# Reordering ScalarE's queue in a cross-attention loop, and moving one projection unit behind each turn of X

## The reference

```python
x = layernorm(x + rwkv_block(x))               # recurrence over the tokens, and a gated MLP
x = layernorm(x + memory_attention(x, ctx))    # one head over causal own tokens and the context
x = layernorm(x + mixture_top1(x))             # 8 experts, 128 -> 512 -> 128
x = layernorm(x + sparse_attention(x))         # 16 heads of 8
x = layernorm(x + cross_attention(x, ctx))     # 16 heads of 64, keys and values from ctx
x = layernorm(x + mixture_top2(x))             # 8 experts with capacity 40
# cross attention:
Q, K, V = proj(x, Wq, bq), proj(ctx, Wk, bk), proj(ctx, Wv, bv)
attn = softmax(einsum('bhqd,bhkd->bhqk', Q, K) / sqrt(64))
out = einsum('bse,de->bsd', einsum('bhqk,bhkd->bhqd', attn, V), Wo)
```

## Time and profile before

| | us |
|---|---|
| three timed runs | 1335.52, 1335.23, 1333.54 |
| their median | 1335.23 |
| the profiled execution, its own time | 1334.87 |
| its span, first to last instruction | 1332.8 |
| mean granted TensorE clock | 0.973 |
| PE busy / DVE busy / ACT busy / POOL busy | 1178.3 / 736.7 / 697.5 / 153.9 |

### The profile page before, as it was taken

The page is one execution under the profiler, slowest core; times in us unless marked ns, Lnnn a source line. Parts: engine busy times, 40 slices in busy tenths (PEclk is TensorE's granted clock), DMA queues, the critical chain, the costliest instruction groups (busy, mean ns, idle before and its releaser), DMA issues.

```text
span 1332.8 us, 21891 instructions
## 1 busy us (share of the span) xinstructions
PE 1178.3 (88%) x7325; PEld 773.1 (58%) x7325; DVE 736.7 (55%) x1890; ACT 697.5 (52%) x1881; POOL 153.9 (12%) x272
## 2 busy tenths in 40 slices
PE   3789989998889998999798999899879999899957
PEld 2563875554765585555485467555467548555536
DVE  5541655667643375657754256566865336555551
ACT  3460765554553285555455157555545418655523
POOL 4310210001120120000212012000022002100000
PEclk9899999999899999999899999999989999999989
DMA  7300000000000000000000000000000000000000
GB/s 232 94 1 0 1 0 1 25 1 1 1 11 1 0 0 1 1 25 1 1 2 10 1 0 1 1 1 25 1 1 9 1 0 0 1 1 1 1 1 8
DMA packets 21058, 15.53 MB, mean 12 GB/s; under 512 B 872, under 2 KB 18645, under 8 KB 20957
## 3 DMA queue, kind: packets, MB, share of 16 engines
q1 hardware_dynamic: 20956, 14.24, 3.7%
HBM read 13.18 MB, written 1.05 MB: 11 GB/s over the span
## 4 chain that ended last, share of the span: by engine, by line
issue 57%; PE 30%; DVE 3%; POOL 3%; ACT 3%; POOLq 1%; SPq 1%; DVEq 0%; DMA 0%; ACTq 0%
PE ps L711 9%; PE ps L783 4%; PE ps L745 3%; PE ps L751 3%; PE ps L803 2%; PE ps L791 2%; POOL rstd L1424 2%; PE ps L724 1%; PE ps L613 1%; PE ps L779 1%; PE ps L646 1%; POOLq L1423 1%; PE ps L695 1%; SPq L440 1%; DVE lg_nmax L1706 1%
## 5 line engine op out<-in xcount | busy, mean ns | idle before, releaser
L1075 ACT ACTIVATE arena<-ps 128x512 f32<-128x512 f32 (+6 forms) x304 | 171.1, 573 | 267.8 <-PE ps L875 207.6
L1856 DVE TENSOR_REDUCE nmax<-ps 128x1 f32<-128x512 f32 x256 | 164.5, 686 | 128.5 <-PE ps L864 128.5
L1266 ACT ACTIVATE arena<-ps,nmax 128x512 f32<-128x512 f32 x256 | 174.3, 686 | 8.0 <-DVE nmax L1856 8.0
L875 PEld LDWEIGHTS ps<-ident,arena 128*128 128x128 f32 x1024 | 109.6, 141 | 110.7 <-issue 63.7
L875 PE MATMUL ps<-ident,arena 128*128 128x128 f32 x1024 | 151.8, 284 | 24.5 <-ACT arena L1266 24.4
L1861 DVE COPY arena<-ps 128x512 f32<-128x512 f32 x128 | 87.7, 685 | 57.3 <-PE ps L875 57.0
L711 PE MATMUL ps<-big,w1a 128*128 128x512 f32 x256 | 117.3, 604 | 0.0
L1235 ACT ACTIVATE arena<-ps,snm 128x136 f32<-128x136 f32 x256 | 91.7, 374 | 5.8 <-DVE snm L1786 5.8
L1422 POOL TENSOR_TENSOR vare<-mv,eps_ln 128x2 f32<-128x2 f32 x64 | 13.4, 209 | 691.0 <-DVE mv L1535 690.6
L711 PEld LDWEIGHTS ps<-big,w1a 128*128 128x128 f32 x256 | 46.3, 189 | 57.5 <-issue 56.5
L783 PE MATMUL ps<-kT,arena 128*128 128x136 f32 x512 | 77.2, 279 | 0.0
(11 more groups left out here) (350 smaller groups left out, 2140.1 us busy)
## 6 DMA issues: line engine op xcount, KB each, us to landing
ctx<-in_ctx_dram SPq DMA_DIRECT2D x4, 512.0 KB, 4.1
w1a<-in_L_ffn_W_dram SPq DMA_DIRECT2D x1, 2048.0 KB, 9.7
w1b<-in_L_ffn_W_dram SPq DMA_DIRECT2D x1, 2048.0 KB, 11.6
w2b<-in_L_ffn_W_dram SPq DMA_DIRECT2D x8, 256.0 KB, 6.2
X<-in_x_dram SPq DMA_DIRECT2D x4, 256.0 KB, 2.9
out_dram<-Y SPq DMA_DIRECT2D x4, 256.0 KB, 2.4
arena<-in_L_xattn_Wq_dram SPq DMA_DIRECT2D x1, 512.0 KB
arena<-in_L_xattn_Wk_dram SPq DMA_DIRECT2D x1, 512.0 KB
```

The costliest lines, as they stand in the source:

```text
L875: last = pe.transpose(ps[:, 4 + h, k * P:(k + 1) * P], cprob[:, h, k * P:(k + 1) * P], ident[:, :])
L1075: return act.activation(dst, src, ACT.Copy)
L1266: act.activation(cprob[:, h, :], bank(2 * (t % 2) + h), ACT.Exp, bias=nmax[:, s:s + 1], accum_out=rsum[:, j % 2, s:s + 1]).then_inc(c_exp, 1)
L1856: dve.tensor_reduce(nmax[:, s:s + 1], bank(s % 4), AX.X, ALU.max, negate=True)\
```

## The change

It has two parts.

**ACT's queue in the cross loop.** In a step t, `pair` had: wait for both heads' transposes, copy bank 5, exponential of head 0 of the next step, then what the step carries once (spread, queries, `rec_projected`), then the exponential of head 1. It now has: wait for head 0's transposes, exponential of head 0 of the next step, wait for head 1's transposes, copy of bank 5, exponential of head 1, and then what the step carries once.

**One unit behind each turn.** At three turns a unit that PE did before the turn is now issued between the turn's transposes and the wait for `XT`: `project_k(0, 2, 1)` at the first mixture, `project_v(3, 6, 0)` at sparse attention, `project_v(2, 3, 1)` at cross attention. A fourth unit, `project_v(3, 6, 1)`, moves from before the last of these turns to behind the first query projection. ACT's copies of these units move behind `x_turned` (and behind `queries(0)`) in the same way. The order of the units among themselves does not change, nor does any instruction's size or number, and DVE's and POOL's code is untouched.

```diff
@@ PE, memory and mixture_top1 @@
                 project_k(0, 1, 0)
-                keys_read(it, 7, 0)
-                project_k(0, 2, 1)
...
-                turn_x(it, 2, 2)
+                turn_x(it, 2, 2, wait=False)
+                keys_read(it, 7, 0)
+                project_k(0, 2, 1)
+                pe.wait_ge(xT_ready, it * 5 + 2)
                 keys_read(it, 0, 0)
@@ PE, mixture_top1 and sparse_attention @@
                 project_v(4, 5, 1)
-                values_read(it, 1, 1)
-                project_v(3, 6, 0)
...
-                turn_x(it, 3, 3)
+                turn_x(it, 3, 3, wait=False)
+                values_read(it, 1, 1)
+                project_v(3, 6, 0)
+                pe.wait_ge(xT_ready, it * 5 + 3)
                 keys_read(it, 4, 1)
                 values_read(it, 3, 0)
@@ PE, sparse_attention and cross_attention @@
                 project_v(2, 7, 0)
-                project_v(2, 3, 1)
-                project_v(3, 6, 1)
...
-                turn_x(it, 4, 4)
+                turn_x(it, 4, 4, wait=False)
                 project_v(2, 3, 1)
+                pe.wait_ge(xT_ready, it * 5 + 4)
...
                 project_q(it, 0, 7)
+                project_v(3, 6, 1)
                 keys_read(it, 0, 1)
@@ ACT, pair(j), for each t @@
+                        nj, nt = (j, t + 1) if t + 1 < TT else (j + 1, 0)
+                        act.wait_ge(cT_ps, it * (NS * PAIRS) + j * NS + 2 * t + 1)
+                        if nj < PAIRS:
+                            exps(nj, nt, 0)
                         act.wait_ge(cT_ps, it * (NS * PAIRS) + j * NS + 2 * t + 2)
                         copy(cprobT[:, 2 * (t % 2) + 1, :], bank(5)).then_inc(cT_odd, 1)
-                        nj, nt = (j, t + 1) if t + 1 < TT else (j + 1, 0)
                         if nj < PAIRS:
-                            exps(nj, nt, 0)
+                            exps(nj, nt, 1)
                         if t == 0 and j:
                             spread(j - 1, 7)
                         if t == 1 and j + 1 < PAIRS:
                             queries(j + 1)
                         if t == 2 and j == PAIRS - 2 and more_groups:
                             rec_projected(it + 1, 0, 7)
-                        if nj < PAIRS:
-                            exps(nj, nt, 1)
@@ ACT, the units' copies @@
                 keys(it, 0, 1, 0)
-                keys(it, 0, 2, 1)
...
                 x_turned(it, 2)
+                keys(it, 0, 2, 1)
...
                 context_values(it, 4, 5, 1)
-                context_values(it, 3, 6, 0)
...
                 x_turned(it, 3)
+                context_values(it, 3, 6, 0)
...
+                x_turned(it, 4)
                 context_values(it, 2, 3, 1)
+                queries(0)
                 context_values(it, 3, 6, 1)
-                x_turned(it, 4)
-                queries(0)
```

More of the change, by code:

```diff
@@ L672, in memory, with mixture_top1 @@
                 project_k(0, 1, 0)
+            def mixture_top1(it):
+                turn_x(it, 2, 2, wait=False)
                 keys_read(it, 7, 0)
                 project_k(0, 2, 1)
-            def mixture_top1(it):
-                turn_x(it, 2, 2)
+                pe.wait_ge(xT_ready, it * 5 + 2)
                 keys_read(it, 0, 0)
@@ L851, in sparse_attention, with cross_attention @@
                 project_v(2, 7, 0)
+            def cross_attention(it, more_groups=True):
+                turn_x(it, 4, 4, wait=False)
                 project_v(2, 3, 1)
-                project_v(3, 6, 1)
-            def cross_attention(it, more_groups=True):
-                turn_x(it, 4, 4)
+                pe.wait_ge(xT_ready, it * 5 + 4)
                 def scores(j, t):
```

## The result

The changed kernel takes 1314.07 us, median of 4 runs (1312.38 to 1315.41), against 1335.38 us (1333.54 to 1337.05) for the kernel before on the same chip: 0.984 of its time, 95% interval 0.9821 to 0.9859. The forecast was 1314.1 us. Its profiled execution took 1315.41 us with a span of 1313.3, 19.5 less than before; that execution is at the upper end of the runs, and why is part of what follows.

The account below looks back on a forecast made before the run. PE was taken to set the pace, standing still for ACT 1.33 of 15.80 us a pair. Loop 15.2 plus turns 5.6, 20.8 off 1334.87, gave 1314.1 us; range 1307 to 1325.

Parts of the forecast that it names:

- steady pairs: Cross-loop pairs 1 to 4, last group 1 to 6: from 15.80 to 15.18 us, 0.62 saved each, 11.2 in all.
- The loop: Cross loop over all groups: steady pairs, pair 0 and pairs 5 to 7 together save 15.2 us.
- the turns: Three turns of X, first mixture, sparse and cross attention: 0.87, 0.15 and 0.39 us saved, times four groups 5.6.
- wait (1): Step 1, head 1: PE waits 0.65 us for ACT before loading it; forecast to vanish.
- step 3's head 1: PE's start on head 1 in step 3: 2.80 us after step 2's start instead of 3.12, 0.32 saved.
- The lag d: Delay between readiness and start of head 0's exponential, its transposes' wait being on a register instruction: taken as 0.12 us.
- Pairs 5 and 6: In the first three groups, pair 5 saves 0.47 us and pair 6 loses 0.59: 1.4 and -1.8 in all.
- my last rival: Step 3: bank 5's copy, behind an exponential awaiting a row maximum, eats the 0.32; about 1321 us, chance 0.08.
- a free wait: Rival: the wait on ACT costs nothing, d = 0; loop gives 18.5 us, time 1310.8; chance 0.15.
- a costly one: Wait before head 0's exponential priced higher: d = 0.30 gives 1323.7 us, chance 0.09; idle ACT was the slower rival's sign.
- The slower rival: Same wait so costly every loop step pays: 53 us per us of d, 1342 us at d = 0.65; chance 0.05.
- the turns give nothing: Rival: moving units behind the three turns saves nothing, leaving only the loop's 15.2 us: 1319.7 us; chance 0.08.

Follow-up runs that it names:

- three orders of the queue: The changed kernel, 1314.07 us; against it, bank 5's copy first again, 1336.03 us; against it, query copy ahead of head 1's exponential, 1304.37 us.
- three copies: Changed kernel with three one-column copies on ScalarE between the wait for the transposes and head 0's exponential: 1321.97 us.
- the run with both waits on the instruction: Changed kernel with head 0's exponential itself waiting for transposes and row maximum, no wait on a register instruction: 1313.7 us.
- the two kernels with the products: Two overwritten PE products added in pair 7's idle time: to the kernel before, 1334.29 us; to that kernel with only the turns' units moved, 1327.98 us.
- the turns' part alone: Changed kernel with ScalarE's old cross-loop queue, only the units behind the three turns moved: 1333.48 us, then 1331.11 us when run again.
- the single small copy: Changed kernel with one one-column copy on ScalarE between the wait for the transposes and head 0's exponential: 1312.91 us.
- the better kernel without the products: Changed kernel with query and recurrence copies ahead of head 1's exponential, both waits on head 0's exponential, later unit wait at the sparse turn: 1298.92 us.

## Why the prediction was right

- **The bound.** PE sets the pace and ACT's queue makes its small waits: in three orders of the queue, and with three copies as a longer lag, steady pairs came to within 0.1 us of what was worked out before the run (15.16 for 15.18, 15.98 for 15.97, 14.71 for 14.80, 15.57 for 15.6 to 15.7). (The prediction puts no other engine above 55% of the span; DVE is at 55.3%, which changes nothing.)
- **Luck in the total.** That 1314.1 meets 1314.07 to the tenth is chance. The loop was put 0.4 us too low and the turns 0.3, and the base of 1334.87 was 0.5 below the median of 1335.38 that the result is compared with.
- **The steady pair.** 15.18 forecast, 15.16 measured; wait (1) gone, 0.43 ahead of the output projection forecast and 0.44 by the starts (at +5.91 for +5.89), step 3's head 1 at 2.76 for 2.80.
- **The lag d.** 0.12 forecast, 0.08 measured. The size was near, the reason only partly right: the row that I read as the price of a separate wait (0.07 on PE) is not ACT's, where that part is 0.02. The Trainium skill, Perfetto Trace Analysis, "Per-engine timelines", lets such a wait hold the sequencer until the semaphore comes, so that decoding follows it; the sign agrees with the run with both waits on the instruction, 0.02 us.
- **Pairs 5 and 6.** Their sum was -0.12 and with pair 7 it is -0.12 (0.19 - 0.42 + 0.11), but the split was wrong, and that the errors cancel is luck. In pair 5 the late copy of bank 5, my last rival, is there, timeline:

```profile
599.89 0.68 ACT L1269 ACTIVATE arena<-ps,nmax 128x512 f32<-128x512 f32 x1
...
600.55 0.59 ACT L1078 ACTIVATE arena<-ps 128x512 f32<-128x512 f32 x1
...
601.29 1.95 PE L889 MATMUL ps<-arena 128*64 128x256 f32 x16 [0.19 <-ACT arena L1078]
```

  The exponential ahead of it was late not for a row maximum, as the rival had it, but for `rec_turned`'s copy, which ACT began at 599.21 in this step. The forecast's steps for pair 5 don't have that copy.

- **The late copy in steady pairs** did not come: 0.22 of cover was left for the 0.28 worked out. The Trainium skill, TensorE: Matmul & The Clock Gate, "Engine queue depths", calls ScalarE strictly first in, first out; pair 5's row agrees, where the copy behind the exponential makes PE wait 0.19.
- **The turns.** 0.87, 0.15 and 0.39 forecast, 0.85, 0.20 and 0.49 measured.
- **What the forecast did not have** is the clock in pair 7. The profiled execution before had one slow pair 7 (17.69 against 16.68 us), the changed one two (1.37 and 1.17 over the first group's). Without that, loop and turns are 15.6 + 5.9 = 21.5 us, the medians differ by 21.3, and the two profiled spans by only 19.5. Of the 2 us that the spans lack, 1.5 stand in pair 7, and the changed kernel's trace is 0.8 later already at the first copy of XT. The other rivals fell: a free wait would need pairs of 15.06, and a costly one an ACT idle with head 0's transposes long done. The slower rival's slope is real (50 for each us), its price isn't. That the turns give nothing is refuted by the copies of XT and by the two kernels with the products.

## What to carry to other kernels

When an in-order queue feeds the bound engine from two sides, write one period out by hand with each start worked out, and ask of each moved instruction what now stands behind it: leaving the query copy behind head 1's exponential cost this change 0.45 us a pair of a possible gain of 1.1. Judge each half of such a diff alone. And before a part is priced by a difference of medians of a few us, look at the granted clock by stretch, since the same code can lose a us in one place in one execution and not in the next.

## What the runs showed of the hardware

- An idle PE of 1.6 to 1.9 us was followed by the lower clock in 15 of 33 pairs 7, and with most of it filled by overwritten products (0.5 us left) in none of 9 (three traces). Such idle time is not the only thing that a fall can follow: in three traces (the turns' part alone, the single small copy, and the better kernel without the products) the clock also fell in the last group's pair 7, at its last values product, behind a wait of about 0.8 us at that place, and cost 1.4 to 1.7 us.
- An exponential on an idle ACT starts 0.76 behind a step's first load when it carries its wait itself and 0.78 when a register instruction does; a one-column copy starts at 0.69. Such a copy holds the queue 0.11 us though its row says 0.20.
- Before any changed code, the first copy of XT stood anywhere from 64.8 to 67.9 us in the fourteen traces. In the four at 64.8 to 64.9 the granted clock between 40 and 50 us is 0.96 or 0.97, in the other ten 0.67 to 0.78. That alone moves the total by 3 us.
